# The masked bias of an attention kernel, written by ScalarE into the scores' PSUM bank ahead of the matmuls

## The reference

```
xn = layernorm(x);  q = xn @ Wq;  k, v = split(xn @ Wkv)          # a learned null key and value go in front
sim = q @ k^T (scaled; in layer 1 q and k are l2-normalised) + bias[h]   # bias: an input in layer 0,
sim = where(causal or masked, -big, sim)                                 # a small network of i - j in layer 1
out = softmax(sim) @ v @ Wo;   x = x + layernorm(out)
```

## Time and profile before

| | us |
|---|---|
| median of 3 runs | 1286.13 (1285.99 to 1287.75) |
| profiled execution, its own time | 1288.04 |
| its span | 1286.0 |
| PE busy | 1251.9 |
| DVE busy | 1106.4 |
| ACT busy | 817.1 |
| POOL busy | 808.4 |

### The profile page before, as it was taken

How to read it: one execution, slowest core, us unless ns; L and a number is a source line. 1 busy time by engine, 2 the same in 40 slices (tenths; PEclk the granted TensorE clock), 3 DMA queues, 4 the chain that set the end, 5 groups by cost and what they waited for, 6 DMA issues and landing times.

```text
span 1286.0 us, 28005 instructions
## 1 busy us (share of the span) xinstructions
PE 1251.9 (97%) x8456; PEld 1159.3 (90%) x8456; DVE 1106.4 (86%) x2808; ACT 817.1 (64%) x3090; POOL 808.4 (63%) x1382
## 2 busy tenths in 40 slices
PE   5899999999999999999999999999999999999997
PEld 5899998999999999998899999999999999999995
DVE  6788988988888888887888889889888988888986
ACT  3756666656666765666666666666666667666663
POOL 6555444545447866557686766667767667666673
PEclk9899999999999999999999999999999999999998
DMA  8221111111522321327350101101101011011111
GB/s 209 98 77 42 40 36 50 50 40 36 91 75 99 124 99 52 114 71 226 123 181 25 50 33 40 49 24 49 49 25 49 26 47 49 24 49 39 34 34 42
DMA packets 52218, 85.97 MB, mean 67 GB/s; under 512 B 7888, under 2 KB 22256, under 8 KB 51616
## 3 DMA queue, kind: packets, MB, share of 16 engines
q1 hardware_dynamic: 46880, 75.02, 18.5%
q0 software_dynamic: 4128, 9.03, 2.5%
q10 hardware_dynamic: 1120, 0.82, 0.2%
HBM read 57.07 MB, written 27.79 MB: 66 GB/s over the span
## 4 chain that ended last, share of the span: by engine, by line
PE 89%; DVE 4%; issue 2%; POOL 2%; DMA 1%; ACT 1%; SPq 1%; POOLq 0%; DVEq 0%; ACTq 0%
PE bank_y L1831 27%; PE bank_q L1745 16%; PE bank_s L1638 12%; PE bank_q L1638 10%; PE bank_o L1638 10%; PE bank_p L1793 6%; PE bank_t L1682 2%; PE bank_t L1757 2%; PE bank_t L1638 2%; ACT p_raw L990 1%; DMA x_in<-in_x 1%; DMA bias<-in_fside_16xSxS 1%; POOL bias_g L751 0%; SPq L481 0%; DVE s_sb L1416 0%
## 5 line engine op out<-in xcount | busy, mean ns | idle before, releaser
L990 ACT ACTIVATE p_raw<-s_sb,neg_m 128x130 f32<-128x130 f32 (+1 forms) x1024 | 371.7, 367 | 169.3 <-DVE neg_m L1423 165.4
L761 POOL TENSOR_TENSOR p_sb<-p_raw,rden 128x256 f32<-128x256 f32 x256 | 159.4, 623 | 223.4 <-DVE rden L1429 223.0
L751 POOL TENSOR_TENSOR bias_g<-bias,mask_row 128x260 f32<-128x260 f32 x256 | 179.6, 702 | 65.2 <-DVE s_sb L1416 64.1
L1831 PE MATMUL bank_y<-wo_h,ot_h 128*128 128x512 f32 x512 | 218.5, 427 | 0.7 <-DVE ot_l L1439 0.7
L1831 PE MATMUL bank_y<-wo_h,ot_l 128*128 128x512 f32 x512 | 203.3, 397 | 0.0
L1831 PE MATMUL bank_y<-wo_l,ot_h 128*128 128x512 f32 x512 | 203.0, 397 | 0.0
L990 ACT ACTIVATION_READ_ACCUMULATOR p_raw<-s_sb,neg_m 128x1 f32 x1024 | 193.5, 189 | 0.0
L1433 DVE TENSOR_TENSOR pt_l<-bank_p,pt_h 128x384 fp32r<-128x384 f32 x256 | 140.8, 550 | 48.0 <-ACT pt_h L997 47.9
L997 ACT ACTIVATE pt_h<-bank_p 128x384 fp32r<-128x384 f32 x256 | 123.3, 482 | 55.8 <-PE bank_p L1793 55.4
L1638 PE MATMUL bank_q<-xt_h,wq_h 128*128 128x256 f32 x512 | 150.1, 293 | 1.7 <-DVE xt_l L1305 1.7
L1416 DVE TENSOR_TENSOR s_sb<-bank_s,bias_g 128x392 f32<-128x392 f32 x256 | 141.8, 554 | 10.1 <-ACT p_raw L990 7.5
(11 more groups left out here) (165 smaller groups left out, 3594.9 us busy)
## 6 DMA issues: line engine op xcount, KB each, us to landing
x_res<-in_x SPq DMA_DIRECT2D x32, 256.0 KB, 2.8
x_mid<-y_out SPq DMA_DIRECT2D x32, 256.0 KB, 2.0
x_in<-x_mid SPq DMA_DIRECT2D x32, 256.0 KB, 2.7
x_res<-x_mid SPq DMA_DIRECT2D x32, 256.0 KB, 2.7
out_x<-y_out SPq DMA_DIRECT2D x32, 256.0 KB, 2.0
x_in<-in_x SPq DMA_DIRECT2D x30, 256.0 KB, 3.2
wq_raw<-in_L_cond_Wq SPq DMA_DIRECT2D x4, 768.0 KB, 6.6
wq_store<-w_sb SPq DMA_DIRECT2D x6, 384.0 KB, 3.8
```

The lines of the kernel that those rows point to most:

```text
L751: e.tensor_tensor(low_blocks(to), low_blocks(of), mask_row[:, :].unsqueeze(1).broadcast_to([P, 2, LOW]), ALU.add)
L761: e.tensor_tensor(to[:, 0:2 * P].rearrange("p (e j) -> p e j", e=2), low_blocks(of)[:, :, 2:LOW], r[:, 0:2, :].broadcast_to([P, 2, P]), AL ...
L990: last = e.activation(p_raw[:, g % 2, lo:hi], s_sb[:, g % 2, lo:hi], ACT.Exp, bias=neg_m[:, h:h + 1], accum_out=esum[:, h:h + 1])
L1831: last = e.matmul(bank_y[:, :], a[:, c, :], b[:, c, :], start=(c == 0 and k == 0), stop=(c == OC - 1 and k == 2))
```

## The change

ACT copies `bias_g` into the scores' bank (`seed`, one instruction of 128 x 392), and the six matmuls of a group run with start=False, so that they add to what lies there. So that the first ones add too, eight matmuls write both banks once at the beginning. DVE's `scores` is gone; maxima and exponentials read the bank, and `s_sb` is dropped. A new semaphore `seeded[g]` stands where `s_ready[g]` was: PE's scores wait for it, and POOL's `masked_bias` does before it writes the buffer again. `seed` waits for the bias of its group and for the exponentials of the group that had the bank. PE issues all waits (`steady` is gone). The lists change: ACT's gets the seeds, PE's `pair` moves some scores behind outputs and projections, POOL's issues `masked_bias` in the order of the groups. The end of POOL's `pair` stays as it was.

```diff
+            def seed(m, g):
+                wait(e, bias_ready[g], m)
+                wait(e, exp_ready[(g + 2) % G], m, -1 if g < 2 else 0)
+                e.activation(bank_s[g % 2][:, 0:GW], bias_g[:, g % 2, :], ACT.Copy).then_inc(seeded[g], 1)
 # exps (ACT)
-                    last = e.activation(p_raw[:, g % 2, lo:hi], s_sb[:, g % 2, lo:hi], ACT.Exp,
+                    last = e.activation(p_raw[:, g % 2, lo:hi], bank_s[g % 2][:, lo:hi], ACT.Exp,
 # masked_bias (POOL)
-                if g == (0 if m[0] == 0 and slot(m) == 0 else 1):
-                    wait(e, mask_ready, m)
-                wait(e, s_ready[(g + 2) % G], m, -1 if g < 2 else 0)
+                wait(e, mask_ready, m)
+                wait(e, seeded[(g + 2) % G], m, -1 if g < 2 else 0)
 # DVE
-            def scores(m, g):
-                wait(e, s_psum[g], m)
-                wait(e, bias_ready[g], m)
-                wait(e, exp_ready[(g + 2) % G], m, -1 if g < 2 else 0)
-                e.tensor_tensor(s_sb[:, g % 2, :], bank_s[g % 2][:, 0:GW], bias_g[:, g % 2, :], ALU.add)\
-                    .then_inc(s_ready[g], 1)
             def maxima(m, g):
-                wait(e, s_ready[g], m)
+                wait(e, s_psum[g], m)
 # scores (PE)
-                if not steady(m) or (g != 2 if second else g > 1):
-                    wait(e, s_ready[(g + 2) % G], m, -1 if g < 2 else 0)
+                wait(e, seeded[g], m)
-                    last = product(out, [(qh, kh), (qh, kl), (ql, kh)])
+                    for a, b in ((qh, kh), (qh, kl), (ql, kh)):
+                        last = e.matmul(out, a, b, start=False, stop=True, skip_group_check=True)
 # ACT, step (one item of layer 1)
                 new(split_xt)
                 on(0, exps, 0)
+                on(0, split_v)
+                on(0, seed, 2)
                 new(q_out, 0)
-                on(0, split_v)
                 on(0, exps, 1)
                 new(q_out, 1)
+                on(0, seed, 3)
                 on(0, exps, 2)
...
                 new(split_kt)
+                on(1, seed, 0)
                 on(0, split_ot, 0)
                 on(0, split_pt, 3)
+                on(1, seed, 1)
 # ACT, pair (two items of layer 0)
                 on(0, exps, 0)
+                on(0, seed, 2)
...
                     on(-1, split_ot, 1)
                     on(3, split_xt)
                     on(0, exps, 1)
+                    on(0, seed, 3)
                 on(0, split_pt, 0)
                 on(0, net_exp)
                 on(0, exps, 2)
+                on(1, seed, 0)
                 on(0, split_v)
                 on(0, split_pt, 1)
                 on(0, exps, 3)
+                on(1, seed, 1)
                 on(0, start_output, 0)
                 on(2, split_group, 1)
                 on(1, high_parts)
                 on(1, exps, 0)
+                on(1, seed, 2)
...
                 on(0, split_pt, 2)
                 on(1, exps, 1)
+                on(1, seed, 3)
...
                 on(4, split_xt)
+                on(2, seed, 0)
                 on(1, split_ot, 0)
                 on(1, split_pt, 3)
+                on(2, seed, 1)
 # POOL, pair
                 on(0, normalise, 1)
-                on(1, masked_bias, 1)
                 on(1, masked_bias, 0)
                 on(0, normalise, 2)
                 on(0, low_part, 1)
+                on(1, masked_bias, 1)
+                on(0, normalise, 3)
+                on(1, masked_bias, 2)
                 on(1, masked_bias, 3)
-                on(1, masked_bias, 2)
-                on(0, normalise, 3)
                 inverse_deviations(event)
 # PE, pair
                 on(-1, attend, 1)
+                on(-1, output, 0, 2)
                 on(0, scores, 2)
-                on(-1, output, 0, 2)
                 on(3, transpose_x)
                 on(-1, output, 2, 4)
                 on(0, scores, 3)
-                on(1, scores, 0)
                 on(0, transpose_p, 0)
                 on(2, project_group, 1)
+                on(1, scores, 0)
                 on(-1, output, 4, 6)
                 on(0, transpose_p, 1)
+                on(-1, output, 6, 8)
                 on(1, scores, 1)
-                on(-1, output, 6, 8)
                 on(0, net_slot)
                 on(2, project_group, 0)
                 on(0, transpose_p, 2)
-                on(1, scores, 3)
                 on(1, scores, 2)
                 on(2, project_kv)
                 on(0, attend, 0)
                 on(0, transpose_p, 3)
+                on(1, scores, 3)
                 on(2, project_group, 3)
```

More of the change, by code:

```diff
@@ L1135, in _ @@
             split_group(first, 1)
+            seed(first, 0)
+            seed(first, 1)
             stream(e, pair, step)
@@ L1666, in transpose_x @@
             def transpose_x(m):
+                wait(e, xn_ready, m)
                 if m[0] == 1:
-                    if not steady(m):
-                        wait(e, xn_ready, m)
                     if opens_layer(m):
@@ L1685, in project_group @@
             def project_group(m, g):
-                if not steady(m) or g == 1:
-                    wait(e, xt_ready, m, 1)
-                if not steady(m) or g > 1:
-                    wait_pair(e, g_ready[(g + 2) % G], m, -1 if g < 2 else 0)
+                wait(e, xt_ready, m, 1)
+                wait_pair(e, g_ready[(g + 2) % G], m, -1 if g < 2 else 0)
                 if is_item(m, 0, 0):
@@ L1722, in transpose_v @@
                 wait_pair(e, vt_copied, m)
[L1723 to L1724 removed]
+                wait_pair(e, pk_ready, m)
                 e.transpose(bank_t[:, 0:P], vt_sb[:, :], ident[:, :]).then_inc(vt_psum, 1)
@@ L1735, in project @@
                     wait(e, xt_ready, m)
-                    if not steady(m):
-                        wait_in_layer1(e, q_done[2], m, -1)
+                    wait_in_layer1(e, q_done[2], m, -1)
                 elif p == 1:
-                    if not steady(m):
-                        wait_in_layer1(e, q_done[1], m, -1)
+                    wait_in_layer1(e, q_done[1], m, -1)
                 else:
@@ L1750, in transpose_q @@
                 if half == 0:
+                    wait_in_layer1(e, q_done[0], m)
                     wait_in_layer1(e, q_done[1], m)
+                    wait(e, xt_ready, m)
                 else:
+                    wait_in_layer1(e, q_done[2], m)
                     wait_in_layer1(e, qt_ready[0], m)
@@ L1788, in transpose_p @@
                 wait(e, p_ready[g], m)
-                if not steady(m) or g > 0 or (m[0] == 0 and slot(m) == 1):
-                    wait(e, pt_ready[(g + 3) % G], m, -1 if g == 0 else 0)
+                wait(e, pt_ready[(g + 3) % G], m, -1 if g == 0 else 0)
                 for k in range(PW // P):
@@ L1796, in attend @@
             def attend(m, half):
-                if not steady(m) or half == 0 or m[0] == 1 or slot(m) == 1:
-                    wait(e, pt_ready[2 * half + 1], m)
-                if not steady(m):
-                    if half == 0:
-                        wait(e, v_ready, m)
-                    if is_item(m, 0, 0) and half == 0:
-                        wait(e, xt_ready, m, 2)
-                    wait(e, ot_ready[1 - half], m, -1 if half == 0 else 0)
+                wait(e, pt_ready[2 * half + 1], m)
+                if half == 0:
+                    wait(e, v_ready, m)
+                if is_item(m, 0, 0) and half == 0:
+                    wait(e, xt_ready, m, 2)
+                wait(e, ot_ready[1 - half], m, -1 if half == 0 else 0)
                 gs = slice(2 * half, 2 * half + 2)
@@ L1823, in output @@
                     e.wait_ge(wo_back[c0 // 4], 32)
-                first_of_pair = m[0] == 0 and slot(m) == 0
-                if c0 == 0 and not (steady(m) and first_of_pair):
+                if c0 == 0:
                     wait(e, y_out_of_psum, m, -1)
-                if c0 == 4 or c0 == 0 and (not steady(m) or first_of_pair):
+                if c0 % 4 == 0:
                     wait(e, ot_ready[c0 // 4], m)
@@ L1912, in pair @@
                 on(0, output, 6, 8)
+            for bank in bank_s:
+                for lo in range(0, GW, P):
+                    width = min(P, GW - lo)
+                    e.matmul(bank[:, lo:lo + width], ident[:, :], ident[:, 0:width], start=(lo == 0), stop=True,
+                             skip_group_check=True)
             first = (0, 0)
```

61 lines of the change are left out of this document (19 added, 42 removed).

## The result

The changed kernel takes 1499.8 us (median of 4 runs, 1496.16 to 1500.38) where the kernel before takes 1286.53 on the same chip: ratio 1.165 [1.164, 1.167], 213 us slower. The prediction said 1464, with a range of 1400 to 1510.

What follows compares the result with a forecast made beforehand. PE was taken as the bound, busy 1251.9 of 1286.0 us. Seam 46.5, inside the pair 54.8 + 5, layer 1 49.3, clock 25.5, less 3, made 178 us: 1288.0 + 178 - 1.9 = 1464, range 1400 to 1510.

Steps and rivals of the forecast that it cites:

- the waits inside the pair: Layer 0, within a pair: PE's scores wait for seeds, 3.65 us a pair, 54.8 in 15 pairs, plus 5 for low_part.
- the clock: After each seam's 3.1 us gap PE runs 3.4 us at 0.50 clock: 15 x 1.7 = 25.5 us.
- Layer 1: Layer 1: PE's scores wait for late seeds, 1.55 us an item, 32 items: 49 us.
- S2: Layer 1, scores of group 2: total late 0.78 us, of which this step adds 0.61.
- S3: Layer 1, scores of group 3: the seed comes behind q_out 1, so PE waits 0.87 us.
- The seam: Layer 0, between two pairs: second scores wait 3.1 us for a bias POOL makes behind rstd; 15 times, 46.5 us.
- S0': Layer 0, first scores of a pair's second item: the chain takes 4.25 us against PE's 3.2, 1.05 late.
- Under 20 us in all: Bound on what the copy's price (0.37 to 0.62 us) could move, over some 75 exposed seeds in layer 0 and 80 in layer 1.
- the dear end: Copy price of 0.62 us where 0.49 was taken: each exposed seed moves by +0.13 us.
- the clock stays up: Rival: the clock isn't lowered over the seams, or only at some: 1439 us, chance 0.2.
- layer 1 hides its seeds: Rival: VectorE without adds runs further ahead, so layer 1 has no waits: 1415 us, or about 1390; chance 0.15.
- More than I count: Rival: the 1 us waits lower the clock too, once or twice a pair, up to 1.7 us each: 1490 to 1515, chance 0.12.

Runs made afterwards that it cites:

- the one POOL position: Changed kernel with POOL making the next pair's group 1 bias ahead of its second rstd instead of behind it: 1457.75 us, ratio 1.134.
- with the maxima: The run of the one POOL position, plus VectorE taking a pair's first maxima ahead of the centring and the layernorm: 1432.13 us, ratio 1.113.
- filling the seams: Changed kernel with 14 matmuls that do nothing between first and second scores at 14 of 15 seams: 1475.72 us; with 26 matmuls 1510.12.
- the reordered kernel: Changed kernel with the same work, but POOL's, DVE's and ACT's lists reordered so that biases, first maxima and seeds come sooner: 1332.64 us, ratio 1.037.
- four pieces of 98: Each seed made as four copies of 98 columns instead of one of 392: 1567.51 us on the changed kernel, 1370.27 on the reordered kernel.

## Why the prediction was right, and where its sizes were off

**The mechanism was right.** PE waits for ACT's copy, the copy for POOL's bias, at the places named. PE's busy share is 88% (85% said), DVE's busy time fell by 121 us, ACT's rose by 80, not 120, since the four exponentials of a group hold ACT 0.17 us less, 44 us in 256 groups. The sum said 178 us and 213 were measured; most of the 35 that lack are in two terms, the waits inside the pair and the clock.

**Layer 1** was taken as 0.17 + 0.61 + 0.87 - 0.1 = 1.55 us an item. Measured: 0.22 + 0.44 + 0.97 - 0.16 = 1.47. 47 us instead of 49. S2 was taken too late and S3 too early, so the sum is a little better than its terms.

**The seam** was taken as 46.5 us, 15 times 3.1. Measured are 49.2 recorded, 51.6 with the 0.16 a wait that the profile leaves out. POOL's second bias instruction took 0.62 us here, so the two took 1.26 and not 1.1. The experiments add what the term did not say: without this wait another of 1.8 us was next. 42 us came back with the one POOL position, and 25.6 more with the maxima.

**Inside the pair** 54.8 + 5 = 59.8 us were taken. Layer 0's waits on the copy are 122.2 us in 72 waits; without the seams, 73.0 in 57. With what the profile leaves out of each they are 83, so this term was mis-sized by 23. The largest part is S0'. It waited 1.66 us instead of 1.05, since POOL's L761 took 0.92 beside DVE's L1468. In the trace of before the same instruction is L763, 256 times with a mean of 0.402 us and 0.60 at most. The Trainium skill (GPSIMD Engine Reference, Specifications) has GpSimd's access to SBUF shared with VectorE, with contention when VectorE has two SBUF inputs; L1468 is such an instruction (y_out and x_res), and the trace agrees: 0.92 beside it, 0.40 once it was moved. Beside DVE's L1445, whose first input is in PSUM, L761 takes 0.40 too.

**The clock** was taken as 15 x 1.7 = 25.5 us. Measured: 22 more stretches, at most 37 us, and 33 at the 1.5 that filling the seams gave for each. "A 3.1 us gap at each seam should do the same" is borne out by all 15 seams. What the term lacks is the rest: a wait of 2.4 us had a stretch behind it too, in three pairs, and four seams had two stretches and the last one three. Filling the seams alone removed 16 stretches and gave 24 us, so the term is real and has the size of one to two stretches per pair.

**PE's busy time** grew by 70 us, which no term speaks of, but it is no cost of its own. At most 37 are the clock. In layer 1 each item lost 1.47 us with 0.88 of idle, and the other 0.59 x 32 = 19 are the parts of the waits that the profile counts as busy. In layer 0 these are 0.16 or 0.25 us for each of 72 waits, 12.5 in all. Idle and busy together: 142 + 70 = 212 of 213 us.

**"Under 20 us in all" for the price of the copy** was too small a bound. It counted the exposed copies and left out the stretches at half clock that came with the longer waits. With 0.27 us more, 155 exposed copies make 42 us, and the kernel lost 68. At that rate the 0.13 of the dear end would have cost some 33, an estimate from these two numbers.

**The rivals.** That the clock stays up is out (27.6 stretches). That layer 1 hides its seeds is out too (21.32). "More than I count", 1490 to 1515, has the measured 1499.8 in its range, which my sum missed by 36 us. Its mechanism is a small part of it: waits of 1.3 us left the clock up (380.9), and the added stretches are at the seams and behind the three waits of 2.4 us. But waits of 1.66 us had half clock behind them as soon as the seams were gone.

**What stays open:** what makes the low stretch two or three times as long at some seams, and why the same wait has half clock behind it in one order of stages and not in another; what the changed lists alone cost, since no run has them with the bank freed by the add as before; and, of the 47 us of the reordered kernel, how much no order could hide. In layer 1 PE had no idle time before, so every wait adds to the time there.

## What to carry to other kernels

Moving an operand from behind a matmul to ahead of it removes an add from one engine, and puts the operand's whole chain of producers in front of PE. Ask of every producer first what it is queued behind (167 of 213 us here), and then what it costs (68 us for 0.27 more a copy). Where PE is the bound, each wait costs itself (a little more than the profile records), and it can bring a stretch at half clock, which the length of that one wait alone doesn't tell. When one wait is removed, look for the next one in the same place before counting the gain.

## What the runs showed of the hardware

- ScalarE copies 392 fp32 columns from SBUF into PSUM in 495 ns, and holds the engine for 0.42 us. The Trainium skill (ScalarE: Activation LUTs, What ACT_TABLE_LOAD costs) gives 186 ns + 0.833 ns an element, with 93 ns overlap between neighbours. An estimate by it is 513 and 420 ns, and for four pieces of 98 a hold of 4 x 175 = 0.70 us; the traces agree on both holds, 0.42 and 0.70 us, and the length is 495 ns, 18 less.
- The exponentials from PSUM take 346 ns in the mean and four hold ACT for 1.27 us; from SBUF 367 ns and 1.44 us.
- The maximum over 260 columns takes 417 ns from PSUM, as much as from SBUF (0.42 in the earlier trace rows).
- An fp32 matmul of 128 x 128 with 128 columns that is no transpose is recorded as two, and takes 0.22 us.
- A POOL instruction of 128 columns took 0.92 us instead of 0.40 beside a DVE instruction with two inputs in SBUF (15 times, 0.85 to 0.92). Beside DVE's layernorm (L1320) it took 0.58 to 0.60.
- PE's recorded idle time is short of what a wait costs by 0.16 us, or 0.25 behind a transpose, since a matmul that doesn't wait begins that long before the recorded end of the one ahead of it.
- Half clock followed all 15 waits of 3.1 to 3.4 us, and a wait of 1.66 us in 1, 3 or 9 of 14 pairs, depending on the order of stages around it.
